# VectorE's order in an attention step: the fourth maximum of the scores behind the third reciprocal and the scaling of the queries

## What is computed

```
ln_out = _ln(hidden_states, ln_w, ln_b)
q  = _ln(_fp8_linear_pertensor(ln_out, wq, ...).reshape(b, s, g, hpg, d), qln_w, qln_b)
k  = _ln(_fp8_linear_pertensor(ln_out, wk, ...), kln_w, kln_b);  v = _fp8_linear_pertensor(ln_out, wv, ...)
core = _gqa(q, k, v)            # softmax(q k^T / sqrt(d)) v
qx = _ln(_fp8_linear_pertensor(ln_out, wqx, ...), ...);  kx, vx = split(cond @ w_kv_x^T)
xout = _gqa(qx, kx, vx)
catq = _div_clamp_fp8(concatenate([core, xout]), proj_smooth)
return einsum('bsi,oi->bso', catq, wproj) * (proj_in_scale * proj_w_scale)
```

## Time and profile before

| | us |
|---|---|
| three runs, median (lowest to highest) | 798.79 (796.70 to 799.75) |
| the profiled execution | 796.67 |
| its span (first to last instruction) | 794.90 |
| busy in it: TensorE / its weight loads | 717.0 / 584.5 |
| busy in it: VectorE, ScalarE, GpSimd | 604.7, 466.3, 448.1 |

### The profile page before, as it was taken

One profiled execution on the slowest core, in us unless ns is written; L12 is line 12 of the kernel. 1 busy time (PEld: TensorE's weight loads), 2 busy tenths in 40 slices (PEclk: granted clock), 3 DMA queues, 4 the chain that ended last, 5 costly groups with the idle time before them and its releaser, 6 DMA issues.

```text
span 794.9 us, 15421 instructions
## 1 busy us (share of the span) xinstructions
PE 717.0 (90%) x4913; PEld 584.5 (74%) x4913; DVE 604.7 (76%) x1286; ACT 466.3 (59%) x1179; POOL 448.1 (56%) x585
## 2 busy tenths in 40 slices
PE   3748899899999989999998999998978799999996
PEld 3646787778888778888886878877856666777775
DVE  6867888788898869788887888888888783454444
ACT  5646867677686766768677676866655232222221
POOL 2425777566767756677776667776866315222220
PEclk9979999999999999999999999999999999999999
DMA  6310100100001010001001010000002015666661
GB/s 186 113 54 1 33 23 1 54 28 28 1 27 29 1 54 28 27 1 28 28 2 52 3 34 2 27 1 2 1 1 61 21 48 148 192 194 190 189 186 54
DMA packets 44479, 42.76 MB, mean 54 GB/s; under 512 B 3717, under 2 KB 43386, under 8 KB 44410
## 3 DMA queue, kind: packets, MB, share of 16 engines
q1 hardware_dynamic: 41706, 36.61, 15.1%
q0 software_dynamic: 1536, 5.28, 2.5%
q10 hardware_dynamic: 1168, 0.01, 0.1%
HBM read 39.52 MB, written 2.37 MB: 53 GB/s over the span
## 4 chain that ended last, share of the span: by engine, by line
PE 63%; DVE 18%; ACT 7%; issue 6%; POOL 4%; ACTq 1%; DMA 0%; POOLq 0%; DVEq 0%
PE out_ps L1760 8%; PE s_ps L1531 7%; PE proj_ps L1487 6%; PE pT_ps L1540 6%; PE proj_ps L1472 6%; PE aux_ps L1550 5%; PE aux_ps L1564 5%; DVE q_tok L1103 5%; PE aux_ps L1501 4%; PE proj_ps L1463 4%; POOL rstd L528 3%; PE work_ps L1752 3%; DVE ss L1083 2%; PE work_ps L1774 2%; PE aux_ps L1408 2%
## 5 line engine op out<-in xcount | busy, mean ns | idle before, releaser
L543 POOL TENSOR_SCALAR p_sb<-p_sb,psum_row 128x256 f32<-128x256 f32 x256 | 125.5, 507 | 67.6 <-DVE psum_row L1122 66.3
L798 ACT ACTIVATE p_sb<-s_ps,negmax 128x256 f32<-128x256 f32 x256 | 118.5, 473 | 64.0 <-DVE negmax L1117 62.8
L1550 PE MATMUL aux_ps<-pT_sb,v_sb 128*128 128x512 f32 x256 | 120.7, 593 | 4.0 <-DVE pT_sb L1128 4.0
L1531 PE MATMUL s_ps<-kT,qT 128*128 128x256 f32 x768 | 112.3, 289 | 8.2 <-DVE qT L1113 4.6
L1128 DVE COPY pT_sb<-pT_ps 128x512 f32<-128x512 f32 x128 | 87.6, 685 | 41.2 <-PE pT_ps L1540 40.5
L550 POOL TENSOR_TENSOR y_bf<-y_bf,mg_bf 128x512 bf16<-128x512 bf16 x64 | 85.9, 1342 | 58.4 <-DVE mg_bf L1140 58.3
L1531 PEld LDWEIGHTS s_ps<-kT,qT 128*128 128x128 f32 x768 | 97.6, 190 | 18.3 <-issue 18.3
L1117 DVE TENSOR_REDUCE negmax<-s_ps 128x2 f32<-128x512 f32 x128 | 86.4, 683 | 5.9 <-PE s_ps L1531 5.6
L528 POOL TENSOR_TENSOR rstd<-var,minus_half 128x8 f32<-128x8 f32 (+1 forms) x64 | 85.7, 1339 | 5.3
L553 POOL TENSOR_TENSOR catq<-y_bf,mg_bf 128x512 fp32r<-128x512 bf16 x64 | 79.6, 1243 | 5.0
L1564 PE MATMUL aux_ps<-wpT,catq 128*128 128x256 f32 x512 | 69.1, 288 | 5.9 <-DVE wkvT L1031 4.8
(11 more groups left out here) (188 smaller groups left out, 1394.9 us busy)
## 6 DMA issues: line engine op xcount, KB each, us to landing
w_up_a<-in_L_ffn_gate_up_proj SPq DMA_DIRECT2D x16, 384.0 KB, 3.5
w_up_b<-in_L_ffn_gate_up_proj SPq DMA_DIRECT2D x16, 384.0 KB, 3.6
wp_raw<-in_L_xattn_wproj SPq DMA_DIRECT2D x16, 256.0 KB, 2.9
w_down_a<-in_L_ffn_down_proj SPq DMA_DIRECT2D x16, 192.0 KB, 3.7
w_down_b<-in_L_ffn_down_proj SPq DMA_DIRECT2D x16, 192.0 KB, 3.6
w_raw<-in_L_xattn_w_kv_x SPq DMA_DIRECT2D x8, 256.0 KB, 4.6
w_raw<-in_L_xattn_wq SPq DMA_DIRECT2D x7, 256.0 KB, 2.7
w_raw<-in_L_xattn_wqx SPq DMA_DIRECT2D x7, 256.0 KB, 3.0
```

Of the source, the lines that this page charges most:

```text
L543: ins = nc.gpsimd.tensor_scalar(p_sb[:, r, st, :], p_sb[:, r, st, :], rsum[:, r, st:st + 1], 1.0, ALU.mult, ALU.mult)
L798: ins = nc.scalar.activation(p_sb[:, r, st, :], s_ps[:, r % 2, st, :], ACT.Exp, bias=negmax[:, r, st:st + 1], accum_out=psum_row[:, r, st: ...
L1531: ins = nc.tensor.matmul(s_ps[:, k % 2, st, :], qT[:, a, ty, h, st * P:(st + 1) * P], kT[:, b, ty, s.gi, :], start=(i == 0), stop=(i == 2))
L1550: ins = nc.tensor.matmul(aux_ps[:, f.bank, :], v_sb[:, (2 * s.n + tt) % VRING, ty, s.gi, :], pT_sb[:, ty, :, tt, :], start=(tt == 0), stop ...
```

## The change

On VectorE, in every step that has a piece to scale and a piece in softmax, `maxes(s1, 3)` moves from ahead of `recip(s1, 2)` to behind `scaled_q(s0)`. The instructions, their operands and the order on all other engines stay as they are; `recip(s1, 3)`, which waits for the fourth exponentials, now follows the maximum directly.

```diff
--- before.py
+++ after.py
@@ -1259,11 +1259,11 @@
                 if i >= 3:
                     add_acc(sub(i - 3))
                 if s1:
-                    maxes(s1, 3)
                     recip(s1, 2)
                 if s0:
                     scaled_q(s0)
                 if s1:
+                    maxes(s1, 3)
                     recip(s1, 3)
                 if i in (NSUB - 1, NSUB):
                     x1_norm(i - NSUB + 1)
```

## The result

The changed kernel takes 834.83 us (median of 4 runs, 833.62 to 835.78) against 797.91 for the kernel before (4 runs, 796.70 to 799.75): a ratio of 1.0455, 95% interval 1.0437 to 1.0474. It is 4.6% slower. The forecast was 830, the range 814 to 842. The profiled execution has a span of 831.8 us, 36.9 longer than before; the sum forecast 32.0.

What follows compares the result with a forecast made beforehand. TensorE's order of work was taken as the bound in the attention steps. Even steps 19.8 plus odd steps 12.2 gave 32.0 us on 796.67, 828.7, or 830.8 against the median; forecast 830, about 4% slower, range 814 to 842.

Steps and rivals of the forecast that it cites:

- The limit of the gain: Scaling of queries on VectorE: cannot start before GpSimd's power ends, so the change gains at most 3.4 us.
- The bank: Even steps: late values' eviction (L812) holds an accumulator bank, TensorE waits at L1513, 12 x 1.4 + 3 x 1.0 = 19.8 us.
- The collision: Odd steps: queries' low part (L1113) issued behind GpSimd's L550 ends 1.89 later; odd-step sum 12.2 us.
- The race: Odd steps: whether L1113 or L550 is issued first; low part forecast 0.45 behind; if it wins, 4.6 us in all.
- without collision: Rival: low part and L550 do not collide, odd steps cost 4.6, time 821 to 824 us; chance 18%.
- with the odd steps only: Rival: TKx does not wait for the bank, or it is freed sooner; some 809 to 811 us; chance 5%.
- faster: Rival: nobody misses the maximum and the waits for `q_tok`, 12.8 us, go; 784 us; chance 3%.
- unchanged: Rival: nobody misses the maximum but the power still holds 14 steps; only 3.4 gained, 793.3 us; chance 6%.
- a gain of 0.26: Steps 7, 15, 23: scaling 0.6 earlier, low part early enough, so each keeps 0.26 us of TensorE's idle time.
- I cost this at nothing: Fourth reciprocal on VectorE waits for late exponentials; next step's first projections cover it on TensorE; without cover 1.7 us.
- takes the whole 1.89: After step 31, where TensorE already waited 1.05, the low part's full 1.89 us delay reaches TensorE.
- the clock: Rival: TensorE's clock falls, each of 28 new stalls costing 0.45 more, 12.6 us in all; 841 to 845 us; chance 6%.

Runs made afterwards that it cites:

- The halves: Against the kernel before, the change made in even steps only: 818.11 us, ratio 1.0261; in odd steps only: 814.87 us, ratio 1.0220.
- the kernel before with values first: Kernel before, with ScalarE evicting the values (L812) ahead of the fourth exponentials, VectorE's order unchanged: 820.39 us, ratio 1.0287.
- only the reciprocal swapped: Kernel before, with the third reciprocal ahead of the fourth maximum and the scaling still behind both: 797.04 us, ratio 1.0000.
- the rounding in halves: Kernel after, with GpSimd's addition L550 split into two halves of 256 columns: 829.62 us, ratio 1.0372.
- the reciprocal behind the copy: Kernel after, with the fourth reciprocal in even steps behind the keys' low part and the third transposed block's copy: 842.09 us, ratio 1.0540.
- the low part first: Kernel after, with VectorE taking the queries' low part (L1113) ahead of the values' clamp and rounding: 842.83 us, ratio 1.0564.
- the mended kernel: Kernel after, values evicted ahead of fourth exponentials and, in even steps, fourth reciprocal behind the third block's copy: 814.87 us; with old order from step 28: 805.34.

## Why the prediction was right, and where it was not

**Right.** *The limit of the gain*: the wait for `q_tok` fell by 2.8 us (at most 3.4 forecast), since the power ends last. *The bank*: 20.1 us, 1.38 in twelve steps and 1.16 in three, against 19.8 from 12 x 1.4 and 3 x 1.0. *The collision*: low parts of 1.56 us in most odd steps, ending within 0.1 of the forecast. The race was closer than forecast, though: L550 led by 0.14 us and not by 0.45, and in step 23 the low part won it by 0.11. *The sum over the steps 1 to 28*: the terms make 26.1 there (17.0 for 13 even steps, 9.1 for 14 odd ones), and 26.7 was measured. The rivals without collision, with the odd steps only, faster and unchanged are out.

**Mis-sized.** The halves show that the 26 was a little too much for the even steps (15.6 measured, 17.0 forecast) and too little for the odd ones (11.2 against 9.1). The steps 7 and 15 were forecast to keep a gain of 0.26, since the low part would be early by 0.6; it took 1.64 and 1.56 there, and they cost 0.50 and 0.42. Only step 23 went as forecast (0.69, and -0.04).

**Wrong: "I cost this at nothing"**, said of the fourth reciprocal's wait, with the next step's projections as cover. In odd steps it holds: with the exponentials late and the values early they cost nothing. In even steps it fails. The cover was looked for on TensorE, but it was VectorE's queue that ran out. In step 16 of before VectorE has 0.22 us of idle time ahead of the low part of the cross keys and 0.53 ahead of the copy of the third block (timeline of before):

```profile
337.43 0.69 DVE L1128 COPY pT_sb<-pT_ps 128x512 f32<-128x512 f32 x1 [0.53 <-PE pT_ps L1540]
```

Against that stands a wait of 1.6 in the kernel before with values first; the 0.9 left over and 0.3 of longer collision (1.64 against 1.35) are the 1.2. The forecast came out right all the same, because the bank wait runs beside it and is as long; the sum needed the longer of the two, once. That is luck, since the prediction did not compare them. And in step 31, which has no projections behind it, the cover that the text names is missing: "takes the whole 1.89" of the collision was the wrong mechanism there. The low part took 0.68 but started 1.43 later (5.30 after the scaling instead of 3.87): behind the reciprocal's wait VectorE has 0.91 us of L1179 in that step, then the copy and the rounding. TensorE stands 1.92 for the fourth block meanwhile, and the scores start 1.44 later.

**Partly come true: the clock.** Of the 36.9 us, 4.9 lie above the sum: 0.6 in the steps 1 to 28, 1.0 ahead of step 1 (the clock is 0.76 from 25 to 60 us, 0.80 before), 1.4 in the steps 28 to 30 (step 28 alone +2.87, where the other even steps had some 1.4) and 1.9 behind step 31. Differences of nearly this size come and go without any cost in the steps: the profiled execution with only the reciprocal swapped has +0.9, +1.3 and +1.2 at these three places, and a span 2.5 longer than before. The rival had the lower level at each of 28 stalls. In this execution it came at none of those of 1.4 us in the steps, but at three places late in the run that have idle times of about 2 us. Timeline of TensorE in the kernel after:

```profile
582.65 1.61 PE L1531 MATMUL s_ps<-kT,qT 128*128 128x256 f32 x6 [2.15 <-DVE qT L1113]
584.06 2.96 PE L1487 MATMUL proj_ps<-wqT,xq 128*128 128x256 f32 x16
...
632.65 0.66 PE L1540 MATMUL pT_ps<-ident,p_sb 128*128 128x128 f32 x4 [1.92 <-POOL p_sb L543]
...
634.44 2.90 PE L1531 MATMUL s_ps<-kT,qT 128*128 128x256 f32 x12 [0.70 <-issue]
...
671.46 1.12 PE L1717 MATMUL work_ps<-ident,mask 128*128 128x128 f32 x4 [2.14 <-DVE mask L1214]
```

The same scores took 1.67 in the kernel before, not 2.90. The prediction set 600 to 635 us against the Trainium skill (TensorE: Matmul & The Clock Gate, section on psum-queue depth-cycling), where frequent short idles make the clock swing. In the kernel after, the steps with an idle of 1.4 disagree with it still (1.00 from 60 to 575 us); the places with 2 us speak for it. Three other kernels speak for it too, and for the rival's condition: with the rounding in halves (steps 2 and 26), the reciprocal behind the copy and the low part first (step 2 in both) the lower level came right at the stall of 1.38 us on the bank. Timeline of TensorE in step 26, first with the rounding in halves (L1515 and L1465 are L1513 and L1463 here), where the granted clock is 0.51 from 533.5 to 537.0 us, then in the kernel after, where it is 1.00:

```profile
533.33 0.86 PE L1515 MATMUL aux_ps<-ident,k_tok 128*128 128x128 f32 x4 [1.38 <-ACT y_bf L814]
533.85 2.05 PE L1465 MATMUL proj_ps<-wkvT,xq 128*128 128x256 f32 x8
```

```profile
537.61 0.63 PE L1513 MATMUL aux_ps<-ident,k_tok 128*128 128x128 f32 x4 [1.39 <-ACT y_bf L812]
538.00 1.20 PE L1463 MATMUL proj_ps<-wkvT,xq 128*128 128x256 f32 x8
```

The step costs 3.13 there instead of 1.59. In these three kernels such a fall costs 1.0 to 1.6 us, more than the 0.45 that the rival set for a stall, but it came at one or two of the 15 stalls and not at each. How much of the 4.3 us outside the steps 1 to 28 is the clock was not measured apart; that the last steps' share goes with their order was, for the mended kernel (805 against 815).

**Left open.** With both chains mended an even step still costs 0.3 to 0.5, and the odd steps shift by +0.7 and -0.7 among themselves; what holds these 6 us was not tried. No kernel here beats the one before.

## What to carry to other kernels

Of an instruction that starts another engine's chain (a maximum that releases exponentials) ask what every engine has queued behind the answer, not only the engine that sets the pace: here a delay of 1.65 us reached TensorE by two ways of nearly equal length, a bank and a queue, and undoing either one gave the even steps nothing back (undoing the queue's also brought on a collision). A wait in the waits view is the last of perhaps several; where the other chains end in the same trace, or a kernel without the wait, shows what stands behind. And a cover counted in a typical step has to be looked for again in the last steps, where the work that made it has run out.

## What the runs showed of the hardware that was not expected

A low part that is issued while L550 runs does not wait for the whole of it: in step 17 it ended 0.55 us after L550's end (374.79 against 374.24), where 0.69 would be its length alone. The Trainium skill (SBUF — State Buffer, section SBUF: two separate sides) has the two exclude each other for the whole instruction; by that it would have ended 0.14 later. The order of issue decides, as the Trainium skill says (same page, section Who interferes with whom): 0.14 us behind L550 gave 1.56, 0.07 behind gave 1.64, and 0.11 ahead of L550 split in two gave 0.69.

The same idle time is followed by either level of the clock: 1.38 and 1.39 us in the rows of step 26 above. So it is with longer ones. In the kernel before, the scores that answer the row at 582.65, and the turns that answer the one at 671.46:

```profile
553.57 0.94 PE L1531 MATMUL s_ps<-kT,qT 128*128 128x256 f32 x6 [2.40 <-DVE qT L1113]
...
635.65 0.66 PE L1717 MATMUL work_ps<-ident,mask 128*128 128x128 f32 x4 [2.13 <-DVE mask L1214]
```

After 2.40 us of idle time the scores ran at full speed here, and after 2.15 at the lower level there; the turns had 2.13 and 2.14 before them and took 0.66 and 1.12. What decides between the two was not found.
